# Attention units: value products of two key tiles together in every second unit

## The chip, the cores and the metric

The kernel runs on one core of one Trainium2 chip. The metric is the device time of one execution in microseconds (us), the median of several runs. Before the change it is 2251.61 us.

## The reference, cut to what matters

`x` is 4 batches of 512 rows by 512 columns, float32. Four layers are added to it in turn: a top-k mask, an attention layer, a recurrent (GRU) layer, and a sampling layer. The change lies in the attention layer:

```python
qkv = (rms_norm(x, g_norm) * (1.0 + scale) + shift) @ W_qkv      # 16 heads of 32
q, k = rms_norm(q, g_q), rms_norm(k, g_k)
logits = einsum('bhqd,bhkd->bhqk', q, k) * d ** (-0.5)
attn = softmax(logits, axis=-1)
o = einsum('bhqk,bhkd->bhqd', attn, v)
x = x + o + o @ W_out
```

## The kernel before, in words

Each engine has a program of its own, written out in order; semaphores tie them together. `pe_attention`, `act_attention` and `dve_attention` run once for each batch b = 0 to 3.

The 16 heads form NC = 4 groups g of HPG = 4 heads, the 512 queries NT = 4 tiles t of P = 128. A *unit* n = 0 to 31 is (g, t, pair): two heads of a group for one tile of queries. So a group of heads is eight units. For a unit the engines do this:

- PE `pe_scores` (line 1989): two products, 128 queries by 512 keys, into banks 2 x pair and 2 x pair + 1. They are issued AHEAD = 2 units early, and wait until the exponentials of unit n - 2 have read the bank.
- DVE `dve_maxima` (line 1425): the row maxima of both heads. POOL multiplies them by the scale (line 561); in batch 3 DVE does it itself (line 1428).
- ACT `act_exponentials` (line 786): two exponentials with row sums.
- PE `pe_turn` (line 2005): four transposes of the first head into bank 4, four of the second into bank 5. Each half waits for its exponential and for the copy that frees the bank: `probs_act` (ACT) for bank 4, `probs_dve` (DVE) for bank 5.
- ACT (line 831) copies bank 4 and DVE (line 1509) copies bank 5 into `probT`.
- PE `pe_weighted_values` (line 2023): for one key tile kt, the products of the four heads of a group with 256 queries (one half of the queries), each head in its own 32 columns of the array (`tile_position`), accumulated over kt = 0 to 3. In the trace each of the four products is two matmuls, so a key tile is eight. The last key tile raises `pv`.

In the unit loop the value products of the half group finished in units 4j to 4j+3 stand one key tile per unit in units 4j+4 to 4j+7. Those of the last half group of the batch stand together behind the loop. After the last key tile of a whole group comes `pe_divide` (line 2038): four transposes of the inverse row sums; ACT copies them (line 793, semaphore `inv_cols`) and DVE multiplies the values by them (line 1436, `out_cols`). The first key tile of the next group waits for `inv_cols`.

The order on the other engines, in unit n: DVE does the maxima of unit n + 2, then (at n = 12, 20, 28) the multiplication of line 1436, then the copy of unit n; at the last unit of a group of heads also a reciprocal (line 1517). ACT does (at n = 12, 20, 28) the copy of line 793, then the copy of unit n, then the exponentials of unit n + 2. On PE unit n is: scores of unit n + 2, transposes of unit n, value products.

Of the kernel before, what the change touches and what calls it, by code (L numbers as in the profile page):

```python
# [18 lines left out]
NT = S // P  # L19
# [23 lines left out]
def values_in_turn(b, t):  # L43

    return b > 0 or t < 2
# [376 lines left out]
HELD = 384  # L422
HAT_SCALE = 2.0 ** 12
VALUES_BANK, DIVIDE_BANK = (6, 7, 6, 7), (7, 6, 7, 6)
TURNED_BANK, NORMED_BANK = (0, 1, 4, 5), (2, 3, 6, 7)
R_BANK, Z_BANK, N_BANK, SIDE_BANK = (0, 3), (1, 4), (2, 5), (6, 7)

# [1430 lines left out]
def pe_places(e, k, b):  # L1858
    s = k.sem
    places = k.bank(6, B, NT)  # L1860
    e.wait_ge(s["equal"], 4 * (b + 1))
    if b == 0:
        e.wait_ge(s["bound"], B * (HIGH_BITS + LOW_BITS))
    elif b > 1:
        e.wait_ge(s["out_cols"], NC * (b - 1))
    e.matmul(places[:, b], k.before[:], k.n_eq[:, b], start=True, stop=False)
    e.wait_ge(s["quota"], 7 * b + 7)
    e.matmul(places[:, b], k.ones[:], k.earlier[:, b], start=False, stop=True).then_inc(s["places"], 1)


def pe_columns(e, k, b):
    s = k.sem
    e.wait_ge(s["masked"], NT * (b + 1))
    if b == 0:
        e.wait_ge(s["bound"], B * (HIGH_BITS + LOW_BITS))
    for c in (0, 1):
        pe_turn_rows(e, k, b, c)
    for c in range(NC):
        pe_norm_rows(e, k, b, c)
    for c in (2, 3):  # L1880
        pe_turn_rows(e, k, b, c)
# [25 lines left out]
def pe_project(e, k, b, t, outputs):  # L1907
    s = k.sem
    n = NT * b + t
    for i in outputs:  # L1910
        bank = 3 * (t % 2) + i
        if t == 0:
            e.wait_ge(s["x_normed"], NC * (b + 1))
            e.wait_ge(s["x_cols"], NC * b + 2)
            if b == 0 and i == 0:
                e.wait_ge(s["w_qkv_in"], 16)
        elif t == 1:
            e.wait_ge(s["x_cols"], NC * (b + 1))
            if b and i:
                e.wait_ge(s[("probs_act", "probs_dve")[i - 1]], len(UNITS) * b)  # L1920
        elif i < 2:
            e.wait_ge(s["qk_rows"], 2 * (n - 2) + i + 1)
        else:
            e.wait_ge(s["values"], n - 1)
        for c in range(NC):
            made = e.matmul(k.bank(bank, D), k.xnT[:, c, t * P:(t + 1) * P], k.w_qkv[:, c, i * D:(i + 1) * D],  # L1926
                            start=(c == 0), stop=(c == NC - 1))
        made.then_inc(s["projected"], 1)


def pe_turn_stack(e, k, b, t, i):
    s = k.sem
    n = TURNS * b + 2 * t + i
    stack = k.stacks_of[b][i]
    e.wait_ge(s["stack_low"], 2 * n + 2)
    for half in range(2):
        to = k.banks[6 + half][:].bitcast(FP16).rearrange("p (h n) -> p h n", h=8)
        if t == i == half == 0 and b + 1 < B:
            e.wait_ge(s["quota"], 7 * (b + 1) + 8)
        if t or i:  # L1940
            e.wait_ge(s[("heads_act", "heads_dve")[half]], n)
        elif b:
            e.wait_ge(s[("inv_cols", "out_cols")[half]], NC * b)
        for h in range(8):
            made = e.transpose(to[:, h], stack[:, half * 8 + h].rearrange("p a d -> p (a d)"), k.ident16[:])  # L1945
        made.then_inc(s["stack_turned"], 1)


def pe_out_matmuls(e, k, b, ms, cs=range(NC)):
    s = k.sem  # L1950
    e.wait_ge(s["out_cols"], NC * b + cs[-1] + 1)
    if b == 0:
        e.wait_ge(s["w_out_in"], 16)
    for m in ms:
        if cs[0]:
            pass
        elif b < B - 1:
            n = NT * (b + 1)
            if m < 2:
                e.wait_ge(s["qk_rows"], 2 * (n + 2) + m + 1)  # L1960
            elif m == 2:
                e.wait_ge(s["values"], n + 3)
            else:
                e.wait_ge(s["qk_rows"], 2 * (n + 3) + 1)
        elif m == 0:
            e.wait_ge(s["exp"], 2 * len(UNITS) * B)
        for c in cs:
            made = e.matmul(k.bank(m, S), k.w_out[:, c, m * P:(m + 1) * P], k.oT[:, c], start=(c == 0), stop=(c == NC - 1))  # L1968
        if cs[-1] == NC - 1:
            made.then_inc(s["w_out"], 1)  # L1970


def pe_scores(e, k, b, n):
    s = k.sem
    g, t, pair = UNITS[n]
    u = len(UNITS) * b + n
    if n == 0:
        e.wait_ge(s["heads_act"], TURNS * (b + 1))
        e.wait_ge(s["heads_dve"], TURNS * (b + 1))
    for i in range(2):  # L1980
        h = g * HPG + 2 * pair + i
        if n >= 2:
            e.wait_ge(s["exp"], 2 * (u - 2) + i + 1)
        elif b:
            e.wait_ge(s["plus_w_out"], NC * (b - 1) + 2 * pair + i + 1)
        elif n == 0:
            e.wait_ge(s["qk_rows"], 2 * NT)
            e.wait_ge(s["values"], NT)
        e.matmul(k.bank(2 * pair + i, S), k.qT[:, h, t * P:(t + 1) * P], k.kT[:, h], start=True, stop=True).then_inc(s["scores"], 1)  # L1989


def pe_turn(e, k, b, n):
    s = k.sem
    g, t, pair = UNITS[n]
    u = len(UNITS) * b + n
    for i in range(2):
        slot, bank = 2 * pair + i, 4 + i
        e.wait_ge(s["exp"], 2 * u + i + 1)
        if n:
            e.wait_ge(s[("probs_act", "probs_dve")[i]], u)  # L2000
        elif i == 0:
            e.wait_ge(s["qk_rows"], 2 * NT * (b + 1))
            e.wait_ge(s["values"], NT * (b + 1))
        for kt in range(NT):
            made = e.transpose(k.bank(bank, NT, P)[:, kt], k.probs[b][:, slot, kt * P:(kt + 1) * P], k.ident[:])  # L2005
        made.then_inc(s["probs_turned"], 1)


def pe_weighted_values(e, k, b, g, half, kt):
    s = k.sem  # L2010
    u = len(UNITS) * b + 8 * g + 4 * half + 4
    queries = slice(half * 2 * P, (half + 1) * 2 * P)
    if kt == 0:
        e.wait_ge(s["probs_act"], u)
        e.wait_ge(s["probs_dve"], u)
        if half == 0:
            if g:
                e.wait_ge(s["inv_cols"], NC * b + g)
            else:
                e.wait_ge(s["heads_act"], TURNS * (b + 1))  # L2020
    for i in range(HPG):
        h = g * HPG + i
        made = e.matmul(k.banks[VALUES_BANK[g]][DH * i:DH * i + DH, queries], k.values[:, kt, h * DH:(h + 1) * DH], k.probT[:, i, kt, queries],  # L2023
                        start=(kt == 0), stop=(kt == NT - 1), tile_position=(0, DH * i))
    if kt == NT - 1:
        made.then_inc(s["pv"], 1)
# [15 lines left out]
def pe_attention(e, k, b):  # L2042
    pe_project(e, k, b, 0, (0, 1, 2))
    if b + 1 < B:
        pe_places(e, k, b + 1)
    for t in range(1, NT):
        pe_project(e, k, b, t, (0,))
        if t > 1:
            pe_turn_stack(e, k, b, t - 2, 1)
        pe_project(e, k, b, t, (1, 2) if values_in_turn(b, t) else (1,))  # L2050
        pe_turn_stack(e, k, b, t - 1, 0)
    if b:
        pe_out_matmuls(e, k, b - 1, (0,))
    else:
        pe_project(e, k, b, NT - 2, (2,))
    pe_turn_stack(e, k, b, NT - 2, 1)
    if b:
        pe_out_matmuls(e, k, b - 1, (1, 2))
    else:
        pe_project(e, k, b, NT - 1, (2,))  # L2060
    pe_turn_stack(e, k, b, NT - 1, 0)
    pe_turn_stack(e, k, b, NT - 1, 1)
    if b:
        pe_out_matmuls(e, k, b - 1, (3,), range(0, 2))
    pe_scores(e, k, b, 0)
    if b:
        pe_out_matmuls(e, k, b - 1, (3,), range(2, NC))
    pe_scores(e, k, b, 1)
    for n, (g, t, pair) in enumerate(UNITS):
        if n + AHEAD < len(UNITS):  # L2070
            pe_scores(e, k, b, n + AHEAD)
        pe_turn(e, k, b, n)
        if n >= 4:
            group, kt = divmod(n - 4, 4)
            pe_weighted_values(e, k, b, group // 2, group % 2, kt)
            if group % 2 == 1 and kt == NT - 1:
                pe_divide(e, k, b, group // 2)
    for kt in range(NT):
        pe_weighted_values(e, k, b, NC - 1, 1, kt)
    pe_divide(e, k, b, NC - 1)  # L2080
    if b + 1 < B:
        pe_columns(e, k, b + 1)
    else:
        pe_out_matmuls(e, k, b, (0, 1), range(NC - 1))
        pe_out_matmuls(e, k, b, (0, 1), range(NC - 1, NC))
        pe_out_matmuls(e, k, b, (2, 3))
# [222 lines left out]
```

## Time and profile before

| | |
|---|---|
| median of 3 runs | 2251.61 us (2249.65 to 2253.29) |
| the profiled execution | 2247.79 us |
| its span | 2246.0 us |
| PE busy | 2129.1 us, 95% |
| DVE busy | 1630.1 us, 73% |
| ACT busy | 1293.8 us, 58% |
| POOL busy | 527.2 us, 23% |

The span runs from the first to the last instruction of one profiled execution. Busy time is the time in which an engine has an instruction in work. A large part of the span, from 733 us on, belongs to the recurrent layer. The unit loops of the four batches lie near 224 to 294, 365 to 438, 508 to 581 and 659 to 731 us. In a row of the timeline, a bracket behind an instruction gives how long its engine had stood idle before it, and the work that ended this. "issue" means that nothing in the profile shows what it waited for.

### The profile page before, as it was taken

How to read it: one execution, taken by the hardware profiler on the slowest of the kernel's cores; microseconds unless marked ns; L12 is line 12 of the kernel's file. 1: busy time of each engine (PE TensorE's matmuls, PEld its weight loads, DVE VectorE, ACT ScalarE, POOL GpSimd, SP SyncE). 2: the span in 40 equal slices, each digit the busy share in tenths (PEclk: the TensorE clock that was granted, in tenths of full speed). 3: DMA queues.
4: the chain of work that ended last, by engine and by line, in shares of the span. 5: the costliest groups of instructions: out<-in, count | busy, mean ns of one | idle time of the engine just before them, and what ended most of it. 6: DMA issues, size and time to landing. Idle time of an engine off the chain costs nothing.

```text
span 2246.0 us, 135671 instructions
## 1 busy us (share of the span) xinstructions
PE 2129.1 (95%) x57232; PEld 1830.8 (82%) x57232; DVE 1630.1 (73%) x6269; ACT 1293.8 (58%) x5763; POOL 527.2 (23%) x2255
## 2 busy tenths in 40 slices
PE   5768999999989999999999999999999999999998
PEld 3654555645545899999999999999999999999997
DVE  7987967878678487777677776667766666766665
ACT  6765947758568345555556655555555545555553
POOL 2002121021120222332233322222222222222221
PEclk8559999999999999999999999999999999999999
DMA  5000000010010000000000000000000000000000
GB/s 208 3 2 1 1 1 1 1 57 1 1 57 1 22 5 5 5 1 1 1 1 1 1 11 1 1 11 1 1 11 1 1 1 10 1 1 11 13 9 14
DMA packets 8410, 26.49 MB, mean 12 GB/s; under 512 B 1028, under 2 KB 1352, under 8 KB 7880
## 3 DMA queue, kind: packets, MB, share of 16 engines
q1 hardware_dynamic: 7712, 23.07, 2.8%
q8 instruction: 135, 2.21, 0.4%
q14 instruction: 139, 1.14, 0.2%
q10 hardware_dynamic: 424, 0.07, 0.0%
HBM read 18.94 MB, written 4.19 MB: 10 GB/s over the span
## 4 chain that ended last, share of the span: by engine, by line
PE 80%; DVE 12%; ACT 4%; issue 2%; DMA 1%; POOL 0%; SPq 0%; DVEq 0%; POOLq 0%; ACTq 0%
PE psum L2257 54%; PE psum L2218 8%; PE psum L2005 3%; PE psum L1926 3%; PE psum L1968 2%; PE psum L2023 2%; PE psum L2103 2%; PE psum L1989 2%; DVE region_cols L1232 2%; DVE region_cols L1248 2%; DVE top L1425 2%; ACT region_rows L786 1%; PE psum L1945 1%; DMA region_cols<-in_L_cond_W_emb_dram 1%; PE psum L1902 1%
## 5 line engine op out<-in xcount | busy, mean ns | idle before, releaser
L2257 PE MATMUL psum<-partsA,region_w_hh 128*128 128x40 f16 x24576 | 855.3, 179 | 10.4 <-issue 4.8
L2257 PE MATMUL psum<-partsB,region_w_hh 128*128 128x40 f16 x24576 | 853.3, 179 | 0.6 <-issue 0.5
L2257 PEld LDWEIGHTS psum<-partsA,region_w_hh 128*128 128x128 f16 x24576 | 758.7, 96 | 37.1 <-issue 11.2
L2257 PEld LDWEIGHTS psum<-partsB,region_w_hh 128*128 128x128 f16 x24576 | 724.1, 96 | 1.1 <-issue 0.5
L599 POOL TENSOR_TENSOR region_w_b<-region_w_b 128x16 f32<-128x16 f32 x1022 | 245.3, 240 | 1078.4 <-DVE region_w_b L1751 1078.4
L1725 DVE TENSOR_REDUCE psum<-psum 128x8 f32<-128x32 f32 x1024 | 201.7, 197 | 198.6 <-PE psum L2257 187.7
L1061 ACT ACTIVATE mixA<-psum 128x8 f32<-128x8 f32 x512 | 95.3, 186 | 428.3 <-DVE psum L1725 428.3
L1075 ACT ACTIVATE region_w_b<-psum 128x8 f32<-128x8 f32 x1024 | 190.0, 186 | 144.0 <-DVE psum L1740 86.9
L601 POOL COPY region_work<-region_w_b 128x8 f32<-128x8 f32 x1024 | 230.9, 225 | 2.2 <-DVE region_w_b L1751 2.2
L1751 DVE TENSOR_TENSOR_SCAN region_w_b<-giveB,region_w_b 128x40 f32<-128x40 f32 x512 | 123.8, 242 | 129.0 <-ACT region_w_b L1075 129.0
L1732 DVE TENSOR_REDUCE psum<-psum 128x8 f32<-128x32 f32 x1024 | 191.1, 187 | 0.7 <-PE psum L2257 0.6
L786 ACT ACTIVATE region_rows<-psum,neg_top 128x512 f32<-128x512 f32 x256 | 174.1, 687 | 28.0 <-POOL neg_top L561 17.4
L1751 DVE TENSOR_TENSOR_SCAN region_w_b<-giveA,region_w_b 128x40 f32<-128x40 f32 x512 | 123.8, 242 | 76.0 <-ACT region_w_b L1075 2.6
L1926 PE MATMUL psum<-region_w_a,region_work 128*128 128x512 f32 x384 | 174.3, 607 | 0.0
L1425 DVE TENSOR_REDUCE top<-psum 128x2 f32<-128x1024 f32 x128 | 156.1, 1222 | 22.4 <-PE psum L1989 22.3
L2218 PE MATMUL psum<-region_cond,region_rows 128*128 x1152 | 171.9, 270 | 0.0
L1068 ACT ACTIVATE giveB<-psum 128x8 f32<-128x8 f32 x512 | 94.9, 185 | 101.7 <-DVE psum L1732 101.5
L2005 PEld LDWEIGHTS psum<-ident,region_rows 128*128 128x128 f32 x1024 | 117.2, 140 | 35.6 <-issue 19.6
L1740 DVE TENSOR_TENSOR_SCAN psum<-mixA,psum 128x32 f32<-128x32 f32 x512 | 117.0, 228 | 35.6 <-PE psum L2257 0.5
L2005 PE MATMUL psum<-ident,region_rows 128*128 128x128 f32 x1024 | 135.6, 274 | 5.4 <-ACT region_work L831 4.5
L1926 PEld LDWEIGHTS psum<-region_w_a,region_work 128*128 128x128 f32 x384 | 72.4, 194 | 83.2 <-issue 82.3
L1740 DVE TENSOR_TENSOR_SCAN psum<-mixB,psum 128x32 f32<-128x32 f32 x512 | 117.2, 229 | 0.2
(265 smaller groups left out, 2820.9 us busy)
## 6 DMA issues: line engine op xcount, KB each, us to landing
region_rows<-in_x_dram SPq DMA_DIRECT2D x4, 1024.0 KB, 11.1
region_w_a<-in_L_cond_W_qkv_dram SPq DMA_DIRECT2D x1, 3072.0 KB, 23.4
region_w_hh<-in_L_cond_W_hh_dram SPq DMA_DIRECT2D x4, 768.0 KB, 6.3
region_w_a<-in_L_cond_W_ih_dram SPq DMA_DIRECT2D x1, 3072.0 KB, 9.9
out_dram<-region_w_b SPq DMA_DIRECT2D x12, 256.0 KB, 2.2
region_cols<-in_L_cond_W_emb_dram SPq DMA_DIRECT2D x1, 2048.0 KB, 19.5
region_cond<-in_cond_dram SPq DMA_DIRECT2D x1, 1024.0 KB, 11.0
region_w_a<-in_L_cond_W_out_dram SPq DMA_DIRECT2D x1, 1024.0 KB, 21.5
```

The costliest lines, as they stand in the source:

```text
L599: e.tensor_tensor(k.line[half][:, :, :, 1:3], new.unsqueeze(3).broadcast_to([P, 2, B, 2]), k.signs.unsqueeze(1).unsqueeze(1).broadcast_to( ...
L601: e.tensor_copy(k.state[:, st + 1, 2 * half:2 * half + 2], new).then_inc(s[f"kept{h}"], 1)
L786: e.activation(k.probs[b][:, 2 * pair + i], k.bank(2 * pair + i, S), ACT.Exp, scale=logit_scale, bias=k.neg_top[:, col + i:col + i + 1], a ...
L1425: e.tensor_reduce(k.top[:, cols], k.psum[:, 2 * pair:2 * pair + 2], AX.X, ALU.max).then_inc(s["top"], 1)
L1725: e.tensor_reduce(k.rz[half][0], k.slots(R_BANK[half])[:, 0], AX.X, ALU.add).then_inc(s[f"rsum{h}"], 1)
L1732: e.tensor_reduce(k.rz[half][1], k.slots(Z_BANK[half])[:, 0], AX.X, ALU.add).then_inc(s[f"zsum{h}"], 1)
L1740: e.tensor_tensor_scan(k.nline[half].rearrange("p c b q -> p (c b q)"), k.mix[half][:].rearrange("p c b q -> p (c b q)"), k.bank(N_BANK[ha ...
L1751: e.tensor_tensor_scan(k.spread[half].rearrange("p c b q -> p (c b q)")[:, 0::2], k.give[half][:].rearrange("p c b q -> p (c b q)"), k.lin ...
L1926: made = e.matmul(k.bank(bank, D), k.xnT[:, c, t * P:(t + 1) * P], k.w_qkv[:, c, i * D:(i + 1) * D], start=(c == 0), stop=(c == NC - 1))
L2005: made = e.transpose(k.bank(bank, NT, P)[:, kt], k.probs[b][:, slot, kt * P:(kt + 1) * P], k.ident[:])
L2218: made = e.matmul(to, stationary, columns, start=False, stop=True, skip_group_check=True)
L2257: made = e.matmul(k.slots(bank)[:, :, ch, :, 0:2], k.w16[:, 2 * read + c, part, NC * "rzn".index(g) + 2 * half + ch], k.parts[read][:, c]. ...
```

## The change

In units 4, 6, 8, ... of a batch PE issues no value products. In units 5, 9, 13, ... (n % 4 = 1) it issues those of key tiles 0 and 1, one behind the other, and in units 7, 11, 15, ... (n % 4 = 3) those of key tiles 2 and 3. `pe_divide` stays behind the last key tile of a whole group, in the same unit as before. The products themselves, their semaphores and the programs of all other engines are unchanged.

```diff
@@ -422,6 +422,7 @@
 VALUES_BANK, DIVIDE_BANK = (6, 7, 6, 7), (7, 6, 7, 6)
+VALUES_TURNS = {1: 0, 3: 2}
 TURNED_BANK, NORMED_BANK = (0, 1, 4, 5), (2, 3, 6, 7)
@@ -2070,9 +2071,10 @@
         pe_turn(e, k, b, n)
-        if n >= 4:
-            group, kt = divmod(n - 4, 4)
-            pe_weighted_values(e, k, b, group // 2, group % 2, kt)
+        if n >= 4 and n % 4 in VALUES_TURNS:
+            group, first = n // 4 - 1, VALUES_TURNS[n % 4]
+            for kt in range(first, first + NT // len(VALUES_TURNS)):
+                pe_weighted_values(e, k, b, group // 2, group % 2, kt)
             if group % 2 == 1 and kt == NT - 1:
                 pe_divide(e, k, b, group // 2)
```

## Rows read from the trace of the kernel before

**Rows 1.** Busy us (count) by stretch: the unit loop of batch 0.
```profile
core 0: us, PE busy (x) PEld busy (x) DVE busy (x) ACT busy (x) POOL busy (x), PEclk, DMA share, GB/s
224.00:294.00 70.00, 66.86 (x599) 41.50 (x599) 59.06 (x74) 62.59 (x162) 8.41 (x35) 1.00 0.01 1
```

**Rows 2.** Timeline (start us, duration us, instruction), PE, one steady unit of batch 0.
```profile
242.10 0.60 PE L1989 MATMUL psum<-region_w_b,region_scratch 128*128 128x512 f16 x2
242.54 1.04 PE L2005 MATMUL psum<-ident,region_rows 128*128 128x128 f32 x8
243.51 0.64 PE L2023 MATMUL psum<-region_work,region_w_b 128*32 128x256 f32 x8
244.08 0.60 PE L1989 MATMUL psum<-region_w_b,region_scratch 128*128 128x512 f16 x2
```

**Rows 3.** Timeline, PE, a unit without value products, batch 1.
```profile
372.08 1.06 PE L2005 MATMUL psum<-ident,region_rows 128*128 128x128 f32 x8 [0.19 <-ACT region_work L831]
372.98 0.74 PE L1989 MATMUL psum<-region_w_b,region_scratch 128*128 128x512 f16 x2
```

**Rows 4.** Timeline, ACT's copies of two units without value products, batch 1.
```profile
373.12 0.64 ACT L831 ACTIVATE region_work<-psum 128x512 f32<-128x512 f32 x1
...
374.93 0.66 ACT L831 ACTIVATE region_work<-psum 128x512 f32<-128x512 f32 x1
```

**Rows 5.** Timeline, PE, the closing four key tiles of batch 0.
```profile
290.50 1.93 PE L2023 MATMUL psum<-region_work,region_w_b 128*32 128x256 f32 x32 [0.31 <-DVE region_work L1509]
292.37 0.66 PE L2038 MATMUL psum<-ident,region_cond 128*128 128x128 f32 x4
```

**Rows 6.** Timeline, DVE, the steady unit of rows 2.
```profile
242.74 1.23 DVE L1425 TENSOR_REDUCE top<-psum 128x2 f32<-128x1024 f32 x1 [0.16 <-PE psum L1989]
...
243.88 0.68 DVE L1509 COPY region_work<-psum 128x512 f32<-128x512 f32 x1
```

**Rows 7.** Timeline, where PE's second half of transposes waited for DVE, batch 1.
```profile
375.71 0.68 DVE L1509 COPY region_work<-psum 128x512 f32<-128x512 f32 x1
...
376.53 0.63 PE L2005 MATMUL psum<-ident,region_rows 128*128 128x128 f32 x4 [0.17 <-DVE region_work L1509]
...
377.09 0.64 PE L2023 MATMUL psum<-region_work,region_w_b 128*32 128x256 f32 x8
```

**Rows 8.** Timeline, batch 0: maxima of unit 6, scores of units 8, 14, 16, 22.
```profile
232.72 1.22 DVE L1425 TENSOR_REDUCE top<-psum 128x2 f32<-128x1024 f32 x1
...
236.16 0.60 PE L1989 MATMUL psum<-region_w_b,region_scratch 128*128 128x512 f16 x2
...
248.53 0.59 PE L1989 MATMUL psum<-region_w_b,region_scratch 128*128 128x512 f16 x2
...
250.30 0.68 DVE L1436 TENSOR_TENSOR region_cond<-psum,region_cond 128x512 f32<-128x512 f32 x1
...
250.90 0.68 DVE L1509 COPY region_work<-psum 128x512 f32<-128x512 f32 x1
...
252.87 0.60 PE L1989 MATMUL psum<-region_w_b,region_scratch 128*128 128x512 f16 x2
...
265.24 0.59 PE L1989 MATMUL psum<-region_w_b,region_scratch 128*128 128x512 f16 x2
```

**Rows 9.** Waits (us in total, times, longest us), 224 to 733 us.
```profile
PE psum L2023 <- ACT region_cond L793: 3.6, 12, 0.3
```

**Rows 10.** Timeline, batch 3: scores of units 14 and 22, DVE in one unit.
```profile
685.59 0.59 PE L1989 MATMUL psum<-region_w_b,region_scratch 128*128 128x512 f16 x2
...
692.75 1.23 DVE L1425 TENSOR_REDUCE top<-psum 128x2 f32<-128x1024 f32 x1
...
694.01 0.16 DVE L1428 TENSOR_TENSOR neg_top<-top,minus_logit_scale 128x2 f32<-128x2 f32 x1
694.09 0.69 DVE L1509 COPY region_work<-psum 128x512 f32<-128x512 f32 x1
...
702.54 0.59 PE L1989 MATMUL psum<-region_w_b,region_scratch 128*128 128x512 f16 x2
```

## The prediction

> **What bounds the kernel now.** I read the busy time by stretches first, then PE's timeline inside the attention unit loop, then DVE's and ACT's timelines at the same instants, and last the waits. The diff only touches the unit loop of `pe_attention`, which runs four times, once per batch. In such a loop PE is busy nearly all the time (66.86 of 70 us), but ACT (62.59) and DVE (59.06) are not far behind [rows 1], so the order in which they hand work to one another matters as much as PE's own sum.
>
> I call the two score products of unit n S(n), its eight transposes T(n) (head pair half 0, then half 1, four each), the value products of one key tile V, DVE's maximum M(n), and DVE's copy of half 1 of the transposes C'(n) (line 1509). ACT copies half 0 (line 831) and does the exponentials. In a steady unit PE starts S at 242.10, T at 242.54, V at 243.51 and the next S at 244.08 [rows 2]: 0.44 + 0.97 + 0.57 = 1.98 us, with no idle time noted on PE. PE sets the pace there. In the first four units of a batch there is no V. PE then has only 0.44 + 0.90 = 1.34 us to do, as T to S takes 0.90 [rows 2, 3]; yet ACT's copies come 1.81 us apart [rows 4] and PE waits 0.19 for one of them in each unit [rows 3]. A unit without V is therefore bound by the other engines at about 1.81, not by PE at 1.34. This is the row to keep in mind, since the change makes every second unit into one without V.
>
> **The change part by part.** Nothing is added or taken away: the same 512 value products stand in another place on PE. Even units (n = 4, 6, ...) lose their V, odd units have two (V2). No queue of DMAs, no instruction of SP or POOL is moved, and `pv` is still raised at the end of units 4k+3, so no buffer is freed in another unit. The first tile of a group stands one unit later, where its semaphores are sooner there.
>
> *The price of V2.* One V costs 0.57 from its start to the next start [rows 2]. Four together cost 292.37 - 290.50 = 1.87 [rows 5]. Each further tile is thus (1.87 - 0.57) / 3 = 0.43, and V2 is 1.00, where two apart are 1.14; that 1.14 is the upper bound. T followed by V takes 0.97 [rows 2], T followed by S 0.90 [rows 3]. On PE alone a pair of units falls from 3.96 to 3.96 - 0.14 - 0.07 = 3.75.
>
> These rows show what entering and leaving the group of narrow products costs, 0.14 + 0.07 = 0.21. The Trainium skill, TensorEngine Tiling (Array Packing), Key Properties, says why such a price exists: changing the tiling mode drains TensorE, while changing the tile does not. By that rule alone this change takes away one change into the mode and one out of it per pair, and the time would fall; it is my first rival below, and the rule speaks against my forecast.
>
> *The loop that closes through DVE.* PE works strictly in order, and four hand-overs now lie in one chain. T(n+1), half 1, waits for C'(n), because there is one bank for it. C'(n) stands on DVE behind M(n+2). M(n+2) needs S(n+2). Take an even unit e; let S(e+2) start at 0, right behind V2.
> - M(e+2) starts 242.74 - 242.10 = 0.64 later [rows 2, 6].
> - C'(e) starts 243.88 - 242.74 = 1.14 behind it [rows 6], at 1.78. (T(e) is no hindrance: it starts at 0.44.)
> - Half 1 of T(e+1) starts 376.53 - 375.71 = 0.82 after the start of that copy [rows 7], at 2.60. PE alone would have been there at 0.44 + 0.90 + 0.44 + 0.45 = 2.23, so it stands 0.37.
> - V2 starts 377.09 - 376.53 = 0.56 behind that half [rows 7], at 3.16.
> - S(e+4) starts 1.00 later, at 4.16.
>
> So a regular pair takes 4.16, against 3.96 now: +0.20. Before the change the same loop asked for only 0.64 + 1.14 + 0.82 = 2.60 from S(n+2) to half 1 of T(n+1), where PE came at 1.98 + 0.44 + 0.45 = 2.87; it was hidden by 0.27 in each unit. Taking V out of the even unit removes 0.57 of that cover, and the idle time it makes cannot be recovered, since the odd unit's V2 is behind the wait in PE's queue, then S(e+4), and DVE's M(e+4) waits for that. ACT is not late: its two units need 2 x 1.81 = 3.62 [rows 4] of the 4.16.
>
> A second estimate, from stretches that exist: an even unit as the units without V run, 1.81, and an odd one as a steady unit with one further tile, 1.98 + 0.43 = 2.41, gives 4.22. I take 4.16, as its steps are all measured between starts on the same chain, and keep 4.22 for the range.
>
> *Where a group of heads ends.* Four transposes (line 2038) come behind the last V of a group. From 236.16 to 248.53 [rows 8] are six units and these: 12.37 - 6 x 1.98 = 0.49, unchanged. In the next even unit DVE also has its division (line 1436) between M and C': it starts 250.30 - 248.53 = 1.77 after S, and the copy 0.60 behind it [rows 8], at 2.37. Half 1 of T follows at 3.19, V2 at 3.75, the next S at 4.75. Now it is 252.87 - 248.53 = 4.34 [rows 8], within which PE waits 0.3 for ACT's line 793, 12 times in all [rows 9]. That wait goes, as V2 asks for it a unit later, but the copy of DVE is late in its place.
>
> A group of eight units, S(14) to S(22), is 265.24 - 248.53 = 16.71 now [rows 8]. After: 4.75 + 3 x 4.16 + 0.49 = 17.72, +1.01, twice per batch. S(8) to S(14): 3 x 4.16 + 0.49 = 12.97 against 12.37, +0.60. The first pair, S(6) to S(8): M(6) starts at 232.72; + 1.14 + 0.82 + 0.56 + 1.00 = 236.24, against 236.16 now [rows 8], +0.08. The last units have no S, and the closing four tiles wait 0.31 for DVE already [rows 5]: part of V2 goes into that idle time. I take +0.1 and bounds of -0.4 and +0.4. A batch: 0.08 + 0.60 + 2.02 + 0.10 = +2.8, and +8.4 for three.
>
> *Batch 3* has one more instruction on DVE, between M and C' (line 1428): M at 692.75, that at 694.01, C' at 694.09 [rows 10], 1.34 in place of 1.14. Its pairs take 4.36. Its group of eight is 702.54 - 685.59 = 16.95 now [rows 10], and 4.95 + 3 x 4.36 + 0.49 = 18.52 after: +1.57, twice. The stretch ahead of it: 13.57 - 12.37 = +1.20; the first pair 0.28, the end 0.1. Together +4.7.
>
> **The sum.** 8.4 + 4.7 = +13.1 us. The profiled execution took 2247.79 (span 2246.0) and would take 2260.9. The three runs have a median of 2251.61, 3.8 above it, and the forecast for the median is 2251.61 + 13.1 = 2264.7.
>
> **The rivals.**
> *Faster: only PE's own sum counts.* It decides if the copy or the maximum of DVE comes early enough, that is if the chain to half 1 of T(e+1) takes no more than 2.23 instead of 2.60. Then each of the 56 pairs saves 0.21, 11.8 us, and the 12 waits for line 793 another 3.6 [rows 9]: 2236.2. For it: PE is at 66.86 of 70 us and its cost falls for certain. Against it: units without V show 1.81 where PE has 1.34 to do [rows 3, 4]. Chance 0.08.
> *No change:* the hand-over from DVE to PE is shorter in this order than 0.82, by some 0.2 (its 0.68-us copy does end earlier), and the pair stays at 3.96. 2251.6, chance 0.10.
> *Slower still:* the pair takes 4.22 as in the second estimate, or V2 costs 1.14 as two single groups do. The first adds 0.06 x 56 = 3.4, the second 0.14 x 56 = 7.8: 2268 to 2272.5. Against the second: four together cost 1.87, not 2.28 [rows 2, 5]. Chance 0.12.
>
> **How the numbers follow.** The forecast has 0.70, the rivals 0.12, 0.10 and 0.08. The likeliest is 2264.7. The range leaves out the two rivals with 0.18 between them: below, the end stretches (4 x 0.5 = 2.0) and 0.08 of 56 pairs (4.5) lead to 2258; above, 2272.5, to 2273. About 0.2% (4.5 us) is what a measurement of this kernel can tell from no change. Slower by more than that: 0.70 + 0.12 = 0.82; within it 0.10; faster 0.08.
>
> **What would show it.** In the changed kernel's PE timeline a regular pair should show V2 of 16 matmuls, 1.00 from start to next S; T(e+1) in two pieces or with idle time ended by DVE's line 1509, in every odd unit, about 0.37 us each; S to S over a pair at 4.16, and 4.36 in batch 3; the idle time ended by line 793 gone. DVE should wait for PE's line 1989 longer than now, once per pair. If pairs run at 3.75, the loop through DVE is wrong; if V2 is 1.14, the price of the switch is.

## The result, and the profile after

The changed kernel takes 2265.47 us (median of 4, 2264.58 to 2269.01), against 2251.41 us for the kernel before in the same comparison (median of 4). The ratio is 1.0064, with a 95% interval of 1.0049 to 1.0079: 14.1 us slower. 13.1 us were forecast.

The page of the changed kernel, busy time per engine:

```profile
span 2264.1 us, 135671 instructions
PE 2135.0 (94%) x57232; PEld 1837.8 (81%) x57232; DVE 1625.9 (72%) x6269; ACT 1289.8 (57%) x5763; POOL 524.9 (23%) x2255
```

The counts are those of before: nothing was added. The time is in the order of the work. This is the timeline of PE over one pair of units of batch 0 (start us, duration us, instruction). One line was added above all these, so line 1989 is now 1990, 2005 is 2006, 2023 is 2024, and 1509 on DVE is 1510.

```profile
241.63 0.60 PE L1990 MATMUL psum<-region_w_b,region_scratch 128*128 128x512 f16 x2
242.07 1.04 PE L2006 MATMUL psum<-ident,region_rows 128*128 128x128 f32 x8
242.95 0.59 PE L1990 MATMUL psum<-region_w_b,region_scratch 128*128 128x512 f16 x2
243.54 1.34 PE L2006 MATMUL psum<-ident,region_rows 128*128 128x128 f32 x8
244.80 1.07 PE L2024 MATMUL psum<-region_work,region_w_b 128*32 128x256 f32 x16
245.81 0.60 PE L1990 MATMUL psum<-region_w_b,region_scratch 128*128 128x512 f16 x2
```

The pair from 241.63 to 245.81 takes 4.18; [rows 2] gave 1.98 for one unit, 3.96 for two. V2 costs 244.80 to 245.81 = 1.01 with its 16 matmuls. The second set of transposes lasts 1.34 in place of 1.04: that is the wait between its halves, which this view merges. It stands open where it is a little longer, and after a group of heads. PE's timeline of batch 1, the unit after line 2038's transposes (now 2039):

```profile
397.20 0.59 PE L1990 MATMUL psum<-region_w_b,region_scratch 128*128 128x512 f16 x2
397.63 1.04 PE L2006 MATMUL psum<-ident,region_rows 128*128 128x128 f32 x8
398.50 0.59 PE L1990 MATMUL psum<-region_w_b,region_scratch 128*128 128x512 f16 x2
399.10 0.63 PE L2006 MATMUL psum<-ident,region_rows 128*128 128x128 f32 x4
400.40 0.63 PE L2006 MATMUL psum<-ident,region_rows 128*128 128x128 f32 x4 [0.67 <-DVE region_work L1510]
400.95 1.07 PE L2024 MATMUL psum<-region_work,region_w_b 128*32 128x256 f32 x16
401.96 0.61 PE L1990 MATMUL psum<-region_w_b,region_scratch 128*128 128x512 f16 x2
```

Half 1 of the transposes waits 0.67 for DVE's copy; S to S is 401.96 - 397.20 = 4.76 (before 4.34, [rows 8]). DVE in the pair that begins at 241.63:

```profile
242.28 1.22 DVE L1426 TENSOR_REDUCE top<-psum 128x2 f32<-128x1024 f32 x1 [0.46 <-PE psum L1990]
243.42 0.68 DVE L1510 COPY region_work<-psum 128x512 f32<-128x512 f32 x1
```

M starts 0.65 behind S, the copy 1.14 behind M, as in [rows 6]; V2 starts 244.80 - 243.42 = 1.38 behind the copy, the 0.82 + 0.56 of [rows 7]. DVE also stands idle for 0.46 ahead of M: PE and DVE wait for each other in turn, and neither is full.

ACT is not far from the same role. Its copy of bank 4 in this pair:

```profile
242.77 0.62 ACT L832 ACTIVATE region_work<-psum 128x512 f32<-128x512 f32 x1
```

Half 0 of T(e+1) starts 0.77 behind it, at 243.54, and 0.59 behind its S, where 0.44 is the rule. From there PE alone would reach V2 0.45 (half of the 0.90) + 0.56 later, at 244.55. So in this pair the wait for DVE's copy costs the last 0.25 us, and without it the pair would take about 3.92, not 3.75 (an estimate from these rows).

The waits between 224 and 750 us (us in total, times, longest) give the sum:

```profile
PE psum L2006 <- DVE region_work L1510: 14.3, 33, 1.0
PE psum L2006 <- ACT region_work L832: 6.2, 22, 0.7
```

Before, PE waited there 0.5 us for line 1509 and 4.5 for line 831. The wait of [rows 9], 3.6 us for line 793, is gone from the list. The time did not stay hidden; the wait for the copy took its place and more. This view counts idle time alone; in a regular pair of batch 1 it has 0.08 ahead of half 1, where the starts show a delay of about 0.3, so the sum is too small. The granted clock of TensorE was 1.00 in all four unit loops from about S(6) on, in both executions, so it has no part in this.

### The profile page after: what moved, and what is told of

Same layout as the page of the kernel before. It is cut to its first block, busy times and chain, and to the rows that moved or that the text cites. A ratio compares the mean times of both kernels' runs of the same rounds, so it can differ in the third digit from the quotient of the medians.

```text
span 2264.1 us, 135671 instructions
## 1 busy us (share of the span) xinstructions
PE 2135.0 (94%) x57232; PEld 1837.8 (81%) x57232; DVE 1625.9 (72%) x6269; ACT 1289.8 (57%) x5763; POOL 524.9 (23%) x2255
## 3 DMA queue, kind: packets, MB, share of 16 engines
q14 instruction: 139, 1.14, 0.2%
## 4 chain that ended last, share of the span: by engine, by line
PE 80%; DVE 13%; ACT 3%; issue 3%; DMA 1%; POOL 0%; SPq 0%; DVEq 0%; POOLq 0%; ACTq 0%
PE psum L2259 53%; PE psum L2220 8%; PE psum L2006 3%; PE psum L1927 3%; PE psum L2024 3%; PE psum L1969 3%; DVE top L1426 2%; PE psum L2105 2%; DVE region_cols L1249 2%; DVE region_cols L1233 2%; PE psum L1990 2%; DVE region_work L1510 1%; PE psum L1946 1%; DMA region_cols<-in_L_cond_W_emb_dram 1%; PE psum L1903 1%
## 5 line engine op out<-in xcount | busy, mean ns | idle before, releaser
L2006 PE MATMUL psum<-ident,region_rows 128*128 128x128 f32 x1024 | 146.3, 278 | 21.9 <-DVE region_work L1510 14.3
```

## The experiments

All kernels were timed beside the kernel before. S to S over a regular pair, and the group of eight from S(14) to S(22), are read from PE's timeline in batch 1.

| kernel | median us | before us | ratio, 95% interval | pair | group of eight, batch 1 |
|---|---|---|---|---|---|
| before | | | | 3.96 | 16.71 |
| changed | 2265.47 | 2251.41 | 1.0064 [1.0049, 1.0079] | 4.17 | 17.77 |
| half_max_before | 2238.89 | 2251.47 | 0.9946 [0.9929, 0.9963] | 3.96 | 16.32 |
| half_max_after | 2241.52 | 2251.47 | 0.9959 [0.9945, 0.9973] | 3.91 | 16.46 |
| values_first | 2257.39 | 2251.47 | 1.0027 [1.0017, 1.0037] | 4.02, one in four 4.51 | 17.26 |
| dve_more_after | 2271.23 | 2251.47 | 1.0089 [1.0073, 1.0106] | 4.31 | 18.31 |
| dve_more_before | 2253.21 | 2249.84 | 1.0017 [1.0007, 1.0026] | 3.96 | 16.83 |
| act_more_after | 2265.54 | 2249.84 | 1.0070 [1.0053, 1.0087] | 4.17 | 17.77 |
| act_more_before | 2250.50 | 2250.20 | 1.0000 [0.9990, 1.0009] | 3.96 | 16.71 |
| two_banks | 2258.23 | 2249.84 | 1.0037 [1.0024, 1.0049] | 3.81 to 4.41 | 17.13 |
| late_half | 2256.13 | 2249.84 | 1.0030 [1.0017, 1.0042] | 3.96, 4.18 to 4.27 | 17.28 |
| pool_last | 2262.78 | 2250.20 | 1.0053 [1.0036, 1.0069] | 4.17 | 17.76 |

### Shorter maxima: does the loop open?

The maxima look at half of the keys; the other half is left out.

```diff
-    e.tensor_reduce(k.top[:, cols], k.psum[:, 2 * pair:2 * pair + 2], AX.X, ALU.max).then_inc(s["top"], 1)
+    e.tensor_reduce(k.top[:, cols], k.psum[:, 2 * pair:2 * pair + 2, 0:S // 2], AX.X, ALU.max).then_inc(s["top"], 1)
```

> The kernel before, but DVE's maxima (line 1425) look at 256 of the 512 keys: the other half of each row is left out of the maximum. The maximum should last about 0.7 us in place of 1.23. Theory (PE sets the pace before, DVE is hidden): a steady pair of units stays at 3.96 us; the kernel gains only where DVE had been late, in batch 3 and at the ends of groups, some 1 to 6 us. Rival (DVE has no part in it at all): within 1 us of before.

> The changed kernel with the same halved maxima. Theory (the loop S(e+2), M(e+2), C'(e), T(e+1) half 1, V2 sets a pair at 4.17 us): with M shorter by 0.5 the copy is bound by T(e) at 1.54 instead, half 1 stands at 2.36, and a regular pair takes 3.92; the added 14 us are gone, and it ends 2 to 6 us below the kernel before with halved maxima. Rival A (two value groups together cost PE more, or the idle time comes from ACT or from PSUM banks of the scores): pairs stay at 4.17, and it stays about 14 us slower than the halved kernel before. Rival B (only part of it is DVE's): in between.

Of the 14.1 us between the two orders, 2241.52 - 2238.89 = 2.6 are left. The maximum lasts 0.69, and the regular pair falls to 3.91 us in the changed order (3.92 forecast), below the 3.96 that PE takes in the old order. So there is a saving on PE, 0.05 of it to be seen here, and the length of M on DVE is what kept it back. The forecast of a gain of 2 to 6 us over the halved kernel before was missed. One cause stands in the unit behind a group of heads. PE and then DVE of half_max_after:

```profile
407.94 0.63 PE L2006 MATMUL psum<-ident,region_rows 128*128 128x128 f32 x4
408.80 0.63 PE L2006 MATMUL psum<-ident,region_rows 128*128 128x128 f32 x4 [0.23 <-DVE region_work L1510]
```

```profile
406.76 0.69 DVE L1426 TENSOR_REDUCE top<-psum 128x2 f32<-128x512 f32 x1 [1.33 <-PE psum L1990]
407.37 0.68 DVE L1437 TENSOR_TENSOR region_cond<-psum,region_cond 128x512 f32<-128x512 f32 x1
407.97 0.68 DVE L1510 COPY region_work<-psum 128x512 f32<-128x512 f32 x1
```

With line 1436 (now 1437) ahead of it the copy is late even behind a short maximum, and that pair takes 4.22 where the halved kernel before takes 3.95. A group of eight is 16.46 against 16.32. The other is the first pair of a batch, S(6) to S(8): 4.83 against 4.47 in batch 1, more than the two groups lose together. The halved kernel before gains 12.6 us on its own, more than the 1 to 6 that I expected. Its trace shows where: from S(6) to the last transposes of a batch (line 2038) it takes 58.98 where before takes 61.14 (batch 1), mostly behind the groups of heads (4.34 to 3.95) and at both ends, and from S(0) to S(6), where there are no value products, 11.14 in place of 11.69. DVE is late in those places before the change, too.

### More work on DVE, more work on ACT

```diff
+        e.tensor_scalar(k.spare[:], k.ident[:], 1.0, None, ALU.mult).then_inc(s["more"], 1)
...
+        e.activation(k.spare_act[:], k.ident[:, 0:8], ACT.Copy).then_inc(s["more"], 1)
```

The first line is that of the two dve_more kernels and stands ahead of the copy of line 1509, the second that of the two act_more kernels and stands behind the copy of line 831. Each waits only for its own instruction of the unit before.

> The changed kernel with one more DVE instruction of about 0.2 us (128x128 copy of the identity into a spare tile) ahead of each unit's copy of line 1509. Theory: it lies in the loop once per pair, so a regular pair goes from 4.17 to about 4.38, about 13 such pairs per batch, 56 x 0.2 = 10 to 12 us more than the changed kernel. Rival (DVE is hidden, ACT or PE bounds the pair): less than 3 us more.

> The kernel before with the same extra DVE instruction as in the run dve_more_after, where it delayed the copy by 0.14 us and the whole kernel by 5.8. Theory: the loop through DVE has 0.27 us of cover in each unit before the change, so regular pairs of batches 0 to 2 stay at 3.96; only units at line 1436 and batch 3 (DVE already at 1.98 per unit) pay, 1.5 to 4 us in all. Rival (the instruction costs alike in both): +5.8.

> The changed kernel with one more ACT instruction (128x8 copy, 0.19 us long) behind each unit's copy of line 831. Theory: ACT has two units of 1.81 in a pair of 4.17 and the loop does not pass through it, so regular pairs stay within 0.03 of 4.17 and the kernel within 2 us of 2265.5. Rival (the exponentials or ACT's copy bound the pair): 0.1 to 0.2 more in each pair, 6 to 11 us.

> The kernel before with the same extra ACT instruction as in act_more_after, where the pairs stayed at 4.17. ACT then has about 1.81 + 0.1 = 1.91 to 2.0 us in a unit of 1.98. Theory: what idle time ACT had in a steady unit takes it, and pairs stay within 0.05 of 3.96; where PE waits for ACT (line 793, first units) it pays, 1 to 4 us in all. Rival (ACT is the bound before as well as PE): 0.1 to 0.2 in each unit, 10 us or more.

DVE of dve_more_after, one even unit:

```profile
392.94 1.21 DVE L1428 TENSOR_REDUCE top<-psum 128x2 f32<-128x1024 f32 x1
...
394.07 0.21 DVE L1508 TENSOR_SCALAR spare<-ident 128x128 f32<-128x128 f32 x1
394.20 0.68 DVE L1514 COPY region_work<-psum 128x512 f32<-128x512 f32 x1
```

The instruction is listed with 0.21, but the copy starts only 0.13 behind it, 1.26 behind M in place of 1.14. A pair takes 4.31 in place of 4.17, so the delay of the copy, 0.12 to 0.13, comes out in the pair in full. The sum is 2271.23 - 2265.47 = 5.8 us: half of what was expected, since the expectation used the listed duration, and twice the size of what a rival without DVE allows (under 3). The same instruction in the kernel before leaves the pairs of batch 1 at 3.96 and costs 3.4 us in all, as expected from the cover of 0.27; batch 3 pays most, with pairs of 4.13 and 4.23.

The instruction on ACT costs nothing that the times show in either: act_more_after has pairs of 4.17 (404.55 to 408.72) and a ratio of 1.0070 where the changed kernel has 1.0064, act_more_before pairs of 3.96 and 0.3 us more than its kernel before. Only the stretch from S(0) to S(6), without value products, is 0.2 longer in both (11.88 in place of 11.68 and 11.69, batch 1), and half of that is made up in the first pair. It is no empty test. ACT of act_more_after, the odd unit:

```profile
403.89 0.59 ACT L834 ACTIVATE region_work<-psum 128x512 f32<-128x512 f32 x1
404.37 0.21 ACT L836 ACTIVATE spare_act<-ident 128x8 f32<-128x8 f32 x1
404.47 0.69 ACT L789 ACTIVATE region_rows<-psum,neg_top 128x512 f32<-128x512 f32 x1
```

The exponential starts 0.58 behind the copy, where the changed kernel has 0.47 (405.48 to 405.95): a delay of 0.11, near that on DVE, and yet the pair stays. ACT's busy time is higher than DVE's in these loops [rows 1], and it is not what sets the pace of a regular pair. That holds for extra work as small as this; by the estimate above, ACT would set it in a pair like the one shown once the wait for DVE were 0.25 shorter.

### A second bank, with nothing left out

```diff
+def spare_bank(n):
+    return n > 4 and n % 2 == 1 and n % 8 != 3
...
+def second_bank(n):
+    return DIVIDE_BANK[(n - 4) // 8] if spare_bank(n) else 5
...
-        slot, bank = 2 * pair + i, 4 + i
+        slot, bank = 2 * pair + i, (4, second_bank(n))[i]
```

> The changed kernel, but in units 8g+5, 8g+7 and 8g+9 the second head's transposes go to a bank that stands free there (the one that takes line 2038's transposes later), so that half 1 of T(e+1) no longer waits for the copy C'(e); nothing is left out. Theory: the pair leaves 4.17 us. PE alone would give 3.75, but with the wait gone the next loop is ACT's: E(e+1), copy of bank 4, half 0 of T(e+1), V2, over two pairs 7.96, thus 3.98 per pair, near the 3.96 of before. Half 1 after line 2038 waits for DVE's multiplication (0.6 sooner than for the copy). 2253 to 2257 in all. Rival (the single bank is not the cause; uneven units or V2 are): pairs stay at 4.17, 2265.

The order is that of the changed kernel; only the bank differs in three of four odd units, and with it the wait: for the copy two units back, or for `out_cols` behind a group of heads. The kernel comes out at 2258.23 us, 1.0037 of before, between the two ends. Its waits, 224 to 750 us:

```profile
PE psum L2020 <- ACT region_work L842: 12.1, 42, 1.3
PE psum L2020 <- DVE region_cond L1447: 2.1, 9, 0.4
PE psum L2020 <- DVE region_work L1520: 1.1, 6, 0.2
```

The wait for the copy of DVE falls from 14.3 to 1.1 us; 5.9 of these 13.2 come back as a wait for ACT's copy of bank 4, which grows from 6.2 to 12.1, and 2.1 as one for the multiplication of line 1436 (here 1447). Here is a wait for ACT, with POOL, ACT and PE in batch 1:

```profile
399.32 0.19 POOL L572 TENSOR_TENSOR neg_top<-top,minus_logit_scale 128x2 f32<-128x2 f32 x1 [2.13 <-DVE top L1436]
399.55 0.69 ACT L797 ACTIVATE region_rows<-psum,neg_top 128x512 f32<-128x512 f32 x1 [0.40 <-POOL neg_top L572]
...
400.23 0.68 ACT L797 ACTIVATE region_rows<-psum,neg_top 128x512 f32<-128x512 f32 x1
...
400.89 0.59 ACT L842 ACTIVATE region_work<-psum 128x512 f32<-128x512 f32 x1
...
401.63 1.06 PE L2020 MATMUL psum<-ident,region_rows 128*128 128x128 f32 x8 [0.18 <-ACT region_work L842]
```

The maxima come late, so the exponentials are late, so ACT's copy is, and PE waits for the bank at the other half. It is the loop that the expectation named, over two pairs. It was put at 3.98 per pair; the pairs measured run from 3.81 to 4.41, with a mean of 4.16 in a group ((17.13 - 0.49) / 4), and the median lies 1.2 us above the forecast of 2253 to 2257. That the single bank binds first is shown; that taking it away does not return the saving is shown too.

### The value products ahead of the transposes

```diff
-        pe_turn(e, k, b, n)
-        if n >= 4 and n % 4 in VALUES_TURNS:
+        if n < 4 or n % 4 not in VALUES_TURNS:
+            pe_turn(e, k, b, n)
+        else:
...
+            pe_turn(e, k, b, n)
```

> The changed kernel, but in the odd units the two key tiles (and line 2038's transposes) stand ahead of the unit's own transposes: order S, V2, T. Theory: V2 then fills the time in which half 1 of T(e+1) waits for DVE's copy. By the same steps half 1 of T(e+1) comes at 3.3 us, long after its release at 2.60; the next wait is half 1 of T(e+2), 0.1 late, and a pair takes 3.88 against 4.17 after and 3.96 before. 0.08 x 56 = 4.5 us below before, and up to 3.6 more for the waits for line 793: 2243 to 2247. Rival (the loss lies in V2 itself or in the uneven units as such, wherever V2 stands): pairs near 4.17, 2265.

With V2 in the place where PE stood idle, 8 of the 14 us come back: 2257.39. The wait of the transposes for the copy of DVE is at 1.3 us in the same view. But the pair takes 4.02, not 3.88, and the kernel stays behind before. PE of values_first:

```profile
381.50 0.59 PE L1990 MATMUL psum<-region_w_b,region_scratch 128*128 128x512 f16 x2
382.01 1.16 PE L2006 MATMUL psum<-ident,region_rows 128*128 128x128 f32 x8
383.01 0.66 PE L1990 MATMUL psum<-region_w_b,region_scratch 128*128 128x512 f16 x2
383.59 1.07 PE L2024 MATMUL psum<-region_work,region_w_b 128*32 128x256 f32 x16
```

S to T is 0.51 (0.44 expected), T to S 1.00 (0.90), S to V2 0.58 (0.44). The first two hold small waits for the copies of the odd unit, which now start later because T stands behind V2. The third has a wait between the two score products (0.66 in place of 0.59 for the two), and the rest, some 0.07, is what T to V also costs over T to S [rows 2, 3]: entering the narrow products, which the steps had left out here.

Those pairs are the smaller part of the loss. Against the kernel before, batch 1 is 1.82 us longer from S(6) to the last transposes, and 1.10 of it lies in the second pair of each group of eight, S(16) to S(18) and S(24) to S(26): 4.51 in place of 3.96. PE there:

```profile
400.53 0.39 PE L1990 MATMUL psum<-region_w_b,region_scratch 128*128 128x512 f16 x1 [0.22 <-ACT region_rows L787]
400.85 1.07 PE L2024 MATMUL psum<-region_work,region_w_b 128*32 128x256 f32 x16
```

The second score product of the odd unit waits for an exponential of ACT, whose bank it takes, and V2 stands behind it. Another 0.49 lies at the end of the batch, where nothing of the value products is left behind the last transposes to fill the wait for DVE's copy (3.5 us for the closing tiles of all batches in the waits, 1.2 before). So V2 in that place takes away the wait for bank 5 and opens others.

### Half of the change, and batch 3

```diff
-VALUES_TURNS = {1: 0, 3: 2}
+VALUES_TURNS = {0: (0,), 1: (1,), 3: (2, 3)}
...
```

> One part of the change alone: key tiles 0 and 1 stand as before, one each in units 4j+4 and 4j+5; key tiles 2 and 3 stand together in units 4j+7, and units 4j+6 have none. Theory: each of these pairs costs what it did in the changed kernel and the others go back to 3.96: 6 pairs per batch, 18 x 0.21 + 6 x 0.39 = +6.1 us over before, 2257.5. Rival (the two halves only cost together, by shifting the whole stream): about 2252; or the whole cost lies in the first two tiles, where line 793 stands.

```diff
-            if b < B - 1:
+            if True:
...
-    if b == B - 1:
...
-        e.tensor_tensor(k.neg_top[:, cols], ...)
```

> The changed kernel, but POOL multiplies the maxima in batch 3 as in the other batches, so DVE no longer has line 1428 between M and C'. Theory: the pairs of batch 3 go from 4.36-4.39 to the 4.17 of the others, its group of eight from 18.59 to 17.77; batch 3 ends 1.7 us sooner. Rival (batch 3 is slower for another reason, such as the weights that are prepared ahead of it): no change in its pairs.

late_half takes 6.3 us more than its kernel before (6.1 expected): the pairs with V2 cost 4.18 to 4.27, the regular ones without it 3.96. The loss is added up pair by pair, and not all of it lies where line 793 stood. The time came as expected, but not by the wait that was expected. PE of late_half in batch 1, the odd unit of a pair with V2, and the waits between 224 and 750 us:

```profile
384.52 1.06 PE L2006 MATMUL psum<-ident,region_rows 128*128 128x128 f32 x8 [0.19 <-ACT region_work L832]
385.51 1.07 PE L2024 MATMUL psum<-region_work,region_w_b 128*32 128x256 f32 x16
```

```profile
PE psum L2006 <- ACT region_work L832: 10.9, 42, 1.0
PE psum L2006 <- DVE region_work L1510: 3.5, 15, 0.4
```

Here all eight transposes wait for ACT's copy of bank 4, and half 1 follows without a wait. That this pair costs 4.18, next to the 4.17 of the changed kernel, is chance: behind a pair with a V in each unit ACT's copy of the even unit starts 1.44 behind S (383.78 - 382.34), in the changed kernel 1.14 (242.77 - 241.63), and it is the last to come. So late_half shows that uneven units cost time one by one; it is no test of the loop through DVE.

In pool_last POOL does the multiplication of line 1428 (the first two lines are in its program), and DVE does not. It brings the group of eight of batch 3 from 18.59 to 17.77 and its pairs to 4.17; it is 12.6 us over its kernel before in place of 14.1. So the dearer pairs of batch 3 come from line 1428 ahead of the copy.

## Why the prediction was right, step by step

**The forecast** was 2264.7 for the median and 2265.47 was measured, in the range of 2258 to 2273, slower as forecast.

**The price of V2**, 1.00 forecast, is 1.00 to 1.01, and T to S is 0.88 (242.07 to 242.95) in place of 0.90. So PE's own saving of some 0.21 per pair stands in the links. No run has a pair at the 3.75 that it would give: half_max_after has 3.91, 0.05 below before, and two_banks 3.81 in its shortest. The rival "only PE's own sum counts" fell by the loop: extra work on DVE lengthens the pair, extra work on ACT does not, and shorter maxima leave 2.6 of the 14.1 us.

**The regular pair**, 4.16 forecast, is 4.17 (241.63 to 249.98, where line 2039's transposes start, are two of them with 8.35). Each link has the length of the row it was taken from. The second estimate, 4.22, was the poorer one. "ACT is not late" was too strong: two of its units fit into a pair, as the forecast summed them, but its copy of bank 4 holds half 0 back by 0.15 in the pair shown above, hidden behind the longer wait of half 1.

**Behind a group of heads**, 4.75 forecast, is 4.76. **A group of eight**, 17.72, is 17.77 (397.20 to 414.97), and the other is the same. **S(8) to S(14)**, 12.97, is 13.01. **The pair of batch 3**, 4.36, is 4.37 to 4.39, and its group of eight 18.59 against 18.52.

**The first pair of a batch** was mis-sized: +0.08 forecast, and +0.43 in batches 1 and 2 (4.94 before, 5.37 after). The step followed only DVE. PE and ACT of the changed kernel in batch 1:

```profile
380.11 0.69 ACT L787 ACTIVATE region_rows<-psum,neg_top 128x512 f32<-128x512 f32 x1 [0.52 <-POOL neg_top L562]
...
381.45 0.59 ACT L832 ACTIVATE region_work<-psum 128x512 f32<-128x512 f32 x1
...
382.19 1.06 PE L2006 MATMUL psum<-ident,region_rows 128*128 128x128 f32 x8 [0.19 <-ACT region_work L832]
...
383.18 1.07 PE L2024 MATMUL psum<-region_work,region_w_b 128*32 128x256 f32 x16
```

There PE waits for ACT's copy of bank 4, 0.74 behind its start, with all eight transposes still to do; DVE's release would have let V2 start at 382.82 by the forecast's steps (381.44 + 0.82 + 0.56), and it started at 383.18, 0.36 later. That is the whole difference. Before, V started as far behind S(6), 379.18 - 374.81 = 4.37, held by the same copy, so the second key tile of V2 came on top with its full 0.43. In batch 0 the first pair grew by 0.63; the further 0.20 is probably from the lower clock ahead of it (last section), since the four executions with a clock of 1.00 there have the same first pair in batch 0 as in batch 1. **The end of a batch**, +0.1, is -0.05 to 0.

**The sum.** From S(6) to the last four transposes of a batch the trace has +3.35, +3.16, +3.16 and +4.81, together 14.5 us, where the steps had 2.8 three times and 4.7. The two profiled executions lie 18.0 us apart, though; 3.5 of that stand outside these stretches (next section but one). The medians, 14.1 apart, agree with the 14.5. The forecast of 13.1 is 1.4 short of the trace, and 1.3 of that are the first pairs (0.5 forecast for the four batches, 1.8 measured).

What is not settled: how much of the 8 us that stay with two_banks is the loop through ACT alone, and what time would be left with both copies in time. Its wait is shown, but the pairs alternate between 3.81 and 4.41, and no run took both copies' waits away at once.

## What to carry to other kernels

An engine that is busy 95% of the time need not be bound by its own sum if it works in order and hands work round a loop: write out the loop with the start-to-start times of its links, and compare it with the engine's own time in each unit. Work that looks like load may be the cover for that loop; bunching it saves a little on the engine and takes the cover away from every second unit. Where two engines are nearly as busy as each other, a small extra instruction on each, one at a time, tells which of them sets the pace; busy time does not, since in the changed order an instruction more on ACT cost nothing and one on DVE cost its whole delay, though ACT was the busier of the two. It tells this of the loop that binds now. The next one can be close behind, as ACT's copy was here, so look in the trace at what each run waits for, and not only at whether its time came as expected.

## What the runs showed of the hardware that was not expected

The granted clock of TensorE just ahead of the first unit loop differs between executions of programs that are equal up to there. Busy time by stretch, first of before, then of the changed kernel (the clock is the third number from the right):

```profile
215.00:232.00 17.00, 10.43 (x78) 6.52 (x78) 14.42 (x21) 13.34 (x29) 1.05 (x6) 1.00 0.00 0
```

```profile
215.00:232.00 17.00, 12.83 (x77) 8.45 (x77) 12.62 (x20) 11.95 (x27) 0.98 (x5) 0.70 0.00 0
```

It was 0.70 in 8 of the 12 profiles, among them half_max_before and dve_more_before, and 1.00 in the others, among them values_first and act_more_after; so it does not follow the change. From 220 to 228 us of the changed kernel it was 0.50, the level of 1.2 GHz, and 1.00, that of 2.4 GHz, in the kernel before; PE has idle times of up to 1.97 us there before and 1.55 us after. From the first scores to S(6) of batch 0 the execution with 0.70 takes 11.80 us and the one with 1.00 takes 10.43. A second stretch, between the unit loops of batches 2 and 3, had a clock of 0.94 and took 79.23 us in the changed kernel (0.66 in 650 to 655 us), against 0.96 and 77.55 us before; that the clock is the cause there is not shown. These 1.4 and 1.7 us are most of what the two profiled executions differ by beyond the change.

A 128x128 instruction on DVE listed with 0.21 us delays the one behind it by 0.12 to 0.13 (dve_more_after), and a 128x8 instruction on ACT listed with 0.21 us delays the one behind it by 0.11 (act_more_after): in these two places the listed duration was more than the price.
